# Scattering the expert rows into the result by an adding DMA, in place of a separate sum at the end of the program

## What is computed

```
logits = x_flat @ gate_w + gate_b;  gates = softmax(logits)
topk_gates, topk_idx = top_k(gates, 2);  topk_gates /= sum(topk_gates)
for e in range(8):
    h = gelu(x_flat @ w1[e] + b1[e]);  y = h @ w2[e] + b2[e]
    out = out + combine[:, e:e + 1] * y
t = t + out          # t: the tokens after the causal attention, "the residual"
```

## Time and profile before

| | us |
|---|---|
| median of three runs | 863.15 |
| lowest and highest of them | 858.99, 865.65 |
| time of the profiled execution | 858.26 |
| its span, first to last instruction | 856.4 |
| tile stage with TensorE full, about | 660 to 836 |
| behind the last scatter's issue | 836.1 to 856.4 |

### The profile page before, as it was taken

How to read it: one execution, slowest core, us unless ns; L and a number is a source line. 1 busy time by engine, 2 the same in 40 slices (tenths; PEclk the granted TensorE clock), 3 DMA queues, 4 the chain that set the end, 5 groups by cost and what they waited for, 6 DMA issues and landing times.

```text
span 856.4 us, 15650 instructions
## 1 busy us (share of the span) xinstructions
PE 737.3 (86%) x5694; PEld 647.3 (76%) x5694; DVE 448.4 (52%) x1073; ACT 333.1 (39%) x724; POOL 156.1 (18%) x306
## 2 busy tenths in 40 slices
PE   4688889989989988998998998878688999999990
PEld 3558778868868867886886887757577999999990
DVE  4355656857667683575767768353534222222213
ACT  6124354333433523344353452423273444444430
POOL 5010000121030220113103022012204121211210
PEclk9999999999999996899999998579798999999995
DMA  6702944931030212203012021955304111111117
GB/s 223 176 11 72 250 108 130 226 94 43 24 89 6 67 38 56 57 11 94 23 46 77 19 57 38 238 151 159 111 7 121 43 39 42 44 42 39 43 34 225
DMA packets 62049, 72.18 MB, mean 84 GB/s; under 512 B 6370, under 2 KB 52286, under 8 KB 61846
## 3 DMA queue, kind: packets, MB, share of 16 engines
q1 hardware_dynamic: 58566, 64.17, 27.7%
q0 software_dynamic: 3408, 7.02, 2.7%
HBM read 27.26 MB, written 23.17 MB: 59 GB/s over the span
## 4 chain that ended last, share of the span: by engine, by line
PE 73%; DVE 9%; DMA 6%; issue 5%; ACT 4%; SPq 1%; POOL 1%; another core or an unknown queue 1%; DVEq 0%; POOLq 0%; ACTq 0%
PE ps L2129 8%; PE ps L1819 7%; PE ps L2112 6%; PE ps L2113 6%; PE ps L1777 5%; PE ps L1778 5%; PE ps L1971 4%; PE ps L1944 4%; PE ps L1995 3%; PE ps L1896 3%; PE ps L1910 3%; DVE max_rows_a L1260 2%; PE ps L2034 2%; DMA q_rows_a<-max_at 2%; PE ps L1863 2%
## 5 line engine op out<-in xcount | busy, mean ns | idle before, releaser
L2112 PE MATMUL ps<-rows_t,w_tile 97*128 97x128 f32 x468 | 91.4, 276 | 3.3 <-DVE rows_t L1488 3.3
L2113 PE MATMUL ps<-rows_t,w_tile 96*128 96x128 f32 x468 | 90.5, 274 | 0.0
L2129 PE MATMUL ps<-w_exp,hid_t 128*128 x468 | 84.2, 331 | 2.3 <-DVE y_out L1496 1.4
L1479 DVE COPY w_tile<-w_exp 96x768 f32 x39 | 21.7, 556 | 120.3 <-PE ps L2113 102.1
L1328 DVE TENSOR_REDUCE max_b<-ps 128x3 f32<-128x384 f32 x96 | 48.6, 549 | 68.9 <-PE ps L2012 67.9
L1819 PE MATMUL ps<-s_q,rel_w 128*128 128x96 f32 x512 | 79.5, 314 | 3.0 <-DMA s_q<-staged_a 1.2
L2129 PEld LDWEIGHTS ps<-w_exp,hid_t 128*128 128x128 f32 x468 | 76.4, 193 | 3.5 <-issue 3.5
L1819 PEld LDWEIGHTS ps<-s_q,rel_w 128*128 128x128 f32 x512 | 74.3, 203 | 5.1 <-issue 2.7
L2112 PEld LDWEIGHTS ps<-rows_t,w_tile 97*128 97x128 f32 x468 | 72.4, 191 | 5.2 <-DVE rows_t L1488 5.1
L881 ACT ACTIVATE probs_a<-ps 98x392 f32<-98x392 f32 x96 | 47.9, 499 | 70.1 <-PE ps L1899 68.3
L2113 PEld LDWEIGHTS ps<-rows_t,w_tile 96*128 96x128 f32 x468 | 70.8, 191 | 0.0
(11 more groups left out here) (229 smaller groups left out, 1633.0 us busy)
## 6 DMA issues: line engine op xcount, KB each, us to landing
xs_dram<-blank SPq DMA_DIRECT2D x32, 388.0 KB, 8.6
w_exp<-in_e_w SPq DMA_DIRECT2D x16, 576.0 KB
ks_a<-staged_a SPq DMA_DIRECT2D x32, 192.0 KB
qs_b<-staged_b SPq DMA_DIRECT2D x32, 192.0 KB
ks_b<-staged_b SPq DMA_DIRECT2D x32, 192.0 KB
tile_x<-xs_dram SPq DMA_DIRECT2D x39, 97.0 KB
w_exp<-y_dram SPq DMA_DIRECT2D x8, 384.0 KB, 6.7
rel_w<-in_rel_tables SPq DMA_DIRECT2D x1, 1792.0 KB, 9.6
```

Of the source, the lines that this page charges most:

```text
L2112: pe.matmul(dst, w1_tile[t % 2][:, 0, cols], rows_t[t % 2][:, 0, :], start=True, stop=False)
L2113: ins = pe.matmul(dst, w1_tile[t % 2][0:DC, 1, cols], rows_t[t % 2][0:DC, 1, :], start=False, stop=True)
L2129: ins = pe.matmul(TILE_Y[:, 0:D], hid_t[t % 2][:, f, :], w_exp[:, bass.ds(e, 1), 2 * MLP + f * D:2 * MLP + (f + 1) * D].rearrange("p e d - ...
```

## The change

The scatter of each tile goes into `result` itself, with addition as the DMA's operation, and `result` has been filled with the residual by `store_t2`. Blank rows have a destination of 2048 or more and are left out by the DMA's bounds check. `t2_dram`, `y_dram`, `t2_all`, `tokens_in` and the whole end are gone. GpSimd's first scatter waits for the stores of the first seven images, and that of tile 21 for all eight. Since a tile must not be added twice, numbers beyond the end now lead to an extra blank tile of `xs_dram`, which takes a 33rd fill, and DVE's `table` does two more operations, for a second table `tile_row` that SyncE reads.

```
-                sp.dma_start(t2_dram[2 * i:2 * i + 2].rearrange("t p d -> p t d"), by_tile(x_4[:, :])).then_inc(t2_out, 16)
+                sp.dma_start(out[2 * i:2 * i + 2].rearrange("t p d -> p t d"), by_tile(x_4[:, :])).then_inc(t2_out, 16)
...
+                        sp.dma_start(xs_dram[NE * TOKENS:], blank[:, :]).then_inc(zero_out, 16)
...
-                at = sp.value_load(tile_at[0:1, t:t + 1], min_val=0, max_val=NE * REGION - 1)
+                at = sp.value_load(tile_row[0:1, t:t + 1], min_val=0, max_val=NE * REGION)
...
-            def tokens_in(t):
-                sp.wait_ge(t2_out, 16 * B)
-                sp.dma_start(t2_all[:, :, :], t2_dram.rearrange("t p d -> p t d")).then_inc(t2_in, 16)
...
-            for q in range(4):
-                for s in range(2):
-                    sp.dma_start(y_all[:, s, quarters[q], :], slots[s, :, quarters[q]]).then_inc(y_in[q], 16)
-            for q in range(4):
-                sp.wait_ge(mixed, q + 1)
-                sp.dma_start(out[quarters[q]].rearrange("t p d -> p t d"), t2_all[:, quarters[q], :]).then_inc(stored, 16)
-            sp.wait_ge(stored, 16 * 4)
+            sp.wait_ge(t2_out, 16 * B)
...
             def tile_out(t):
                 gp.wait_ge(y_sb, t + 1)
+                if t == 0:
+                    gp.wait_ge(t2_out, 16 * (B - 1))
+                if t == EARLY:
+                    gp.wait_ge(t2_out, 16 * B)
                 if t:
                     gp.wait_ge(y_sent[(t - 1) % 2], 16 * ((t - 1) // 2 + 1))
                 gp.indirect_dma_start(
-                    out=y_dram, out_offset=bass.IndirectOffsetOnAxis(
+                    out=out.rearrange("t p d -> (t p) d"), out_offset=bass.IndirectOffsetOnAxis(
                         ap=tile_x[t % RING][:, DEST:DEST + 1].bitcast(U32), axis=0),
-                    in_=y_out[t % 2][:, :], in_offset=None).then_inc(y_sent[t % 2], 16)
+                    in_=y_out[t % 2][:, :], in_offset=None, bounds_check=TOKENS - 1, oob_is_err=False,
+                    compute_op=ALU.add).then_inc(y_sent[t % 2], 16)
...
+                after(dv.tensor_scalar(tile_f[:, lo:hi], tile_f[:, lo:hi], float(NE * REGION), None, ALU.min))
+                dv.tensor_copy(tile_row[:, lo:hi], tile_f[:, lo:hi])
                 after(dv.tensor_scalar(tile_f[:, lo:hi], tile_f[:, lo:hi], float(NE * REGION - 1), None, ALU.min))
...
-            dv.wait_ge(t2_in, 16)
-            for q in range(4):
-                dv.wait_ge(y_in[q], 32)
-                now = slice(NT // 4 * q, NT // 4 * (q + 1))
-                after(dv.tensor_tensor(t2_all[:, now, :], t2_all[:, now, :], y_all[:, 0, now, :], ALU.add))
-                dv.tensor_tensor(t2_all[:, now, :], t2_all[:, now, :], y_all[:, 1, now, :], ALU.add).then_inc(mixed, 1)
```

More of the change, by code:

```diff
@@ L73, in build @@
     pad_scratch = nc.dram_tensor("pad_scratch", (2, DC, 2, WIN), F32, kind="Internal").ap()
-    t2_dram = nc.dram_tensor("t2_dram", (NT, P, D), F32, kind="Internal").ap()
-    xs_dram = nc.dram_tensor("xs_dram", (NE * TOKENS, ROW), F32, kind="Internal").ap()
-    y_dram = nc.dram_tensor("y_dram", (2 * TOKENS + P, D), F32, kind="Internal").ap()
+    xs_dram = nc.dram_tensor("xs_dram", (NE * TOKENS + P, ROW), F32, kind="Internal").ap()
     with ExitStack() as keep:
@@ L82, in sem, with layers @@
             return keep.enter_context(nc.semaphore(name))
-        layers(nc, a, pad_scratch, t2_dram, xs_dram, y_dram, ps, sem, out)
-def layers(nc, a, pad_scratch, t2_dram, xs_dram, y_dram, ps, sem, out):
+        layers(nc, a, pad_scratch, xs_dram, ps, sem, out)
+def layers(nc, a, pad_scratch, xs_dram, ps, sem, out):
     with ExitStack() as ctx:
@@ L157, in layers @@
         tile_at = sb("tile_at", [P, NTILE], I32)
+        tile_row = sb("tile_row", [P, NTILE], I32)
         NORMS = ("a", "m", "b", "g")
@@ L207, in layers @@
             y_out = two("y_out", [P, D])
-            t2_all = sb("t2_all", [P, NT, D])
             tile_x = [sb(f"tile_x{n}", [P, ROW]) for n in range(RING)]
-        y_all = w_exp[:, :, :].rearrange("p e n -> p (e n)")[:, 0:2 * NT * D].rearrange(
-            "p (s t d) -> p s t d", s=2, t=NT)
         slot_rows = probs_a[:, :, :, :].rearrange("p r e n -> p (r e n)")[:, 0:KEYS]
@@ L284, in layers @@
             "twinned", "scattered", "dve_step", "totalled", "tiles_known")
-        w_in, b2_in, t2_in, ones_row = sems("w_in", "b2_in", "t2_in", "ones_row")
+        w_in, b2_in, ones_row = sems("w_in", "b2_in", "ones_row")
         tile_in = [sem(f"tile_in{n}") for n in range(RING)]
@@ L289, in layers @@
             "rows_ps", "rows_sb", "w1_first", "w1_second", "h_ps", "h_sb", "y_ps", "b2_sb", "y_sb")
-        y_in, mixed, stored = [sem(f"y_in{n}") for n in range(4)], sem("mixed"), sem("stored")
         went_on = sem("went_on")
@@ L525, in last @@
                     store_t2(i)
-                tokens_in(0)
                 tile_rows(4)
@@ L567, in _ @@
                 sp.wait_ge(y_sent[u], 16 * ((NTILE + 1 - u) // 2))
-            slots = y_dram[0:2 * TOKENS].rearrange("(s t p) d -> s p t d", s=2, p=P)
-            quarters = [slice(NT // 4 * q, NT // 4 * (q + 1)) for q in range(4)]
-            for q in range(4):
-                for s in range(2):
-                    sp.dma_start(y_all[:, s, quarters[q], :], slots[s, :, quarters[q]]).then_inc(y_in[q], 16)
-            for q in range(4):
-                sp.wait_ge(mixed, q + 1)
-                sp.dma_start(out[quarters[q]].rearrange("t p d -> p t d"), t2_all[:, quarters[q], :]).then_inc(stored, 16)
-            sp.wait_ge(stored, 16 * 4)
+            sp.wait_ge(t2_out, 16 * B)
         @block.gpsimd
@@ L661, in go @@
                     if i == 0 and k == 0:
-                        gp.wait_ge(zero_out, 16 * FILLS)
+                        gp.wait_ge(zero_out, 16 * (FILLS + 1))
                     if k == 0:
@@ L1385, in route_constants @@
                     for slot in range(2):
-                        dv.tensor_scalar(by_slot[:, :, slot], steps[:, :], lane[:, :], float(slot * TOKENS), ALU.add, ALU.add)
-                    after(dv.tensor_scalar(dest_f[:, 4 * B:4 * B + 1], lane[:, :], float(2 * TOKENS), None, ALU.add))
+                        dv.tensor_scalar(by_slot[:, :, slot], steps[:, :], lane[:, :], 0.0, ALU.add, ALU.add)
+                    after(dv.tensor_scalar(dest_f[:, 4 * B:4 * B + 1], lane[:, :], float(TOKENS), None, ALU.add))
                     dv.tensor_copy(dest[:, :], dest_f[:, :]).then_inc(dest_set, 1)
```

## The result

The changed kernel takes **867.71 us** (median of 20 runs, 860.23 to 885.11) beside 859.14 us of the kernel before; the ratio of the two is **1.014, with a 95% interval of 1.011 to 1.018**. 846.7 us and "faster" had been forecast, with a range up to 864. The forecast was wrong in sign.

What follows compares the result with a forecast made beforehand. TensorE, busy 86% of 856.4 us, was taken as the bound. The sum -17.6 + 0.8 + 0.4 = -16.4, applied to the median of 863.15, gave 846.7 us; range 841 to 864.

Steps and rivals of the forecast that it cites:

- The end, -17.6: After the last scatter's landing: all loads, sums and stores go except 0.42 us of leaving the program, 17.6 us less.
- The landing, 3.1: Adding scatter, issue to landing (L): 2.3 us plain plus 0.8 for a reading phase; costs 0.8 once at the tail.
- The ring closes at L = 3.7: Tile stage, four buffers reused: TensorE waits for loaded tiles only once the scatter's landing time L reaches 3.7 us.
- two periods = 5.99 + L: Tile stage: transpose to scatter 3.17, landing L, 0.72 to the load's issue, 2.1 to its landing; against 9.7 us.
- the slack, 1.6 us: Tile stage, kernel before: tile 38's load lands about 1.6 us before TensorE starts its transpose, so the load waits for TensorE.
- rival 2: Tile stage: L between 3.7 and 5.0 gives part back, for instance 861 us at 4.4; chances 0.09 to 4.06, 0.13 beyond.
- Rival 1: Tile stage: slow adding scatter, GpSimd's strict order needing L + 0.3 per tile; worked case 916 us; chance 0.23 above L 5.0.
- The signs that I had named for a wrong L: Next profile: median landing above 3.7, scatter intervals grown by half the excess, TensorE's idle time ended by `tile_x`.
- The tightest place at the beginning: Tile 2's scatter behind image 7's: its buffer is full at 666.5, TensorE wants it at 667.69, 1.2 us of slack.
- The fill: SyncE's queue: one extra DMA of 97 KB in front of 32 larger ones, cost 0.
- the load of 1536 KB: In the middle, beside the routing of image 7: its removal was counted as no gain, 0.
- the 0.4 forecast: DVE's table: two more operations 0.21 us apart, +0.4 us, all on the path.

Runs made afterwards that it cites:

- no_end: Kernel before without its final loads, sums and stores, residual stored into the result, experts' rows missing: 847.9 us beside 861.67, ratio 0.990.
- plain_scatter: Changed kernel with the addition taken out of the scatter, bounds check kept: 855.13 us, kernel before beside it 861.67.
- ring8: Changed kernel with eight tile buffers instead of four: 852.69 us, kernel before beside it 861.67, ratio 0.9985.
- extra_fill: Kernel before with only the 33rd fill of xs_dram added: 859.49 us beside 859.97, ratio 0.9997.
- after_again: Changed kernel, unaltered, timed again in a later set: median 874.6 us of six runs, kernel before beside it 861.67.
- ring6: Changed kernel with six tile buffers instead of four: 846.05 us, kernel before beside it 859.97, ratio 0.985.

## Why the forecast was wrong, step by step

**The end, -17.6: the step "save the 0.42 of leaving the program" was wrong.** Behind the last scatter show only what ended last. GpSimd's drain of 7.07 us was in the trace, under the loads, and I hadn't looked for what the removed work covered. Measured: 20.3 - 7.6 = **12.7**, where the forecast had 16.8 with the 0.8 of the longer landing taken off. no_end shows it without the rest of the change.

**The landing, 3.1: near by luck, 0.4 too small.** Measured 3.5. Half of the added 1.2 us is the longer issue (1.55 for 0.96), which I had only named as a way to be wrong. The DMA slices of 0.2 us from 785 to 793 show the rest:

```profile
DMA  0000466000000968980000030000377200000000
GB/s 0 0 0 0 74 202 198 23 0 0 0 0 0 58 54 104 165 112 0 0 0 0 0 82 0 0 0 0 47 159 233 58 0 0 0 0 0 0 0 0
...
q0 software_dynamic: 144, 0.10, 12.2%
```

The scatter issued at 785.54 has its packets in slices 14 to 18, that is 1.0 us where the earlier trace rows had 0.6. So the packets take 0.4 us more, not the 0.8 of a whole load, and whether that is a phase of reading no trace shows. It makes 144 packets instead of 48, for the same 0.10 MB. The engines work 12.2% of 16 x 8 us = 15.6 us for this one, against 7.1%, or 9.1 us, for two before: 3.4 times as much for one scatter. The rule of the Trainium skill (Collectives: The Full Stack, in "The bandwidth ceiling"), which is stated there for a step of a collective, would have had twice as much. The trace disagrees on both sides: the stretch of packets grew 1.7 times, the engines' time 3.4 times.

**The ring closes at L = 3.7: the step that decided.** The measured L of 3.5 lay below that, where the prediction's own sum has -17.6 + 1.2 + 0.4 = -16.0 and no wait. Two terms were missing from "two periods = 5.99 + L". The first is 0.51 for the bounds check, an edit in the diff that I had given no price. It stands ahead of the issue, and so isn't part of L. The second is 0.75 for TensorE's register load. I measured the slack, 1.6 us, from the load's landing to the *transpose*, and took it for the slack of TensorE. But its sequencer has to be ahead of the matrix unit by the register load behind the transpose; once it is held at the transpose's wait, that load lies open. With both, two periods are 7.25 + L, and the ring closes at L = 9.70 - 7.25 = **2.45 us**, not 3.7. A plain scatter of 2.3 just passes (plain_scatter: 4.85); by this sum 0.15 us more is enough to close the ring. At 3.5 the sum gives 5.37, measured 5.34. Taking off 0.75, 0.5 and both gives 5.0, 5.12 and 4.85; measured were 5.04, 5.21 and 4.95.

**The mechanism of the loss is that of rival 2, the ring of buffers, at a threshold that lay elsewhere; more than the whole gain was given back.** Rival 1's order on GpSimd was put at L + 0.3; with the check's 0.5 it is the 4.3 us at which ring8 catches up, less than 4.85, so it is not the bound. The signs that I had named for a wrong L came in another form: intervals grew, but TensorE's idle time was not ended by `tile_x`.

**The smaller steps.** The tightest place at the beginning had been given 1.2 us of slack, enough for 0.8. There, at the transpose of tile 6, TensorE waited 1.30 us. Tile 2's scatter took 1.91 us to issue, and the load into its buffer was issued 4.54 us behind its start (682.66 to 687.20), not 3.04; and TensorE wanted the buffer sooner, 5.3 us behind that start (689.26 - 1.30 - 682.66) where the rows of before had 6.35. The fill was free (extra_fill), and no_end shows no gain from the load of 1536 KB. In the second table the row copy starts 0.60 us behind the first of the limiting operations (678.66 to 679.26), before 0.29: 0.3 of the 0.4 forecast.

**The new sum.** 181.70 - 165.20 = +16.5 in the 34 intervals, -12.7 at the end: +3.8 from tile 4 on (189.3 - 185.5; 3.3 in after_again). Ahead of it, from SyncE's load of the last row maxima into `qs_b` (620.23 and 641.47) to tile 4's scatter, it is 50.6 before and 52.3 after: +1.7. That makes +5.5, where -16.4 was forecast: 16.5 of the 21.9 us between them are the ring, 4.1 the end, and 1.3 lies ahead of tile 4, as much as TensorE's wait at tile 6. The medians say +8.6, the ratio +9 to +15, the means of all 20 runs +10.9 with 4.1 either way. **What is left, 3 to 10 us, by the means perhaps only 1, stays open.** In the profiled pair it lies in the image stages and goes with their granted clock (0.89 and 0.93). But kernels with the whole change had 0.93 too (ring6), and one without it had 0.90 (no_end), so I can't put it down to the change, nor to the missing idle time at the end. If the stretch from tile 4 on is taken off the mean time of each kernel (three runs above 900 us left out), what lies ahead of it is as long in no_end and in extra_fill as in the kernel before (-0.3 and +0.8), and between -0.9 and +9.2 us longer in the kernels that carry the change, with 4 to 8 either way. So neither the 33rd fill nor the residual's new place shows a cost, and the rest differs too much from kernel to kernel to be given a cause.

**The version that beats both.** The changed kernel with six or eight buffers: 0.985 (0.977 to 0.992) with six from four runs, 0.987 (0.982 to 0.991) and 0.9985 (0.994 to 1.003) with eight in two sets, of which the first gives GpSimd one wait more and the second shows no gain. From tile 4 on it is 14 us shorter than the kernel before, and 18 shorter than the changed one. The space is that of the `t2_all` that the change freed.

## What to carry to other kernels

Before you price a longer transfer, write down the whole loop from one reuse of its buffer to the next, with the waits as the *sequencers* meet them: slack up to the first matmul behind a wait is not slack if a register load stands behind it and has been running ahead. When work at the end of a program is removed, look in the trace for what ran beneath it, an engine's drain too; the end moves to the next cover, not to the last removed line. A ring that is less than a microsecond from closing (here 9.70 - 6.74 - 2.3 = 0.66, where the prediction had 1.4) turns a gain of 13 us into a loss. Two more buffers settle it, and one register load moved ahead of a wait takes 10 of the 16.5 us back.

## What the runs showed of the hardware that I had not expected

- An adding indirect scatter of 128 rows of 768 bytes occupies GpSimd for 1.55 us (plain: 0.96) and lands after 3.5 us (plain: 2.3), in 144 packets instead of 48.
- The bounds check adds 0.5 us between the releasing semaphore and the issue (0.78 to 0.80 against 0.27 to 0.28) and leaves the issue as it is (0.98 against 0.96).
- GpSimd's drain at the end of the program takes 7.1 us when it starts with a plain scatter, 7.65 with an adding one, and 5.9 when all has landed. In all eleven kernels without the old end, the span ends 0.2 to 0.3 us behind it.
- Adding scatters that wait for each other follow at 4.3 us (ring8). The last interval, behind a blank tile, is 3.6 there.
- The load of the expert number takes TensorE's sequencer 0.8 us, and 0.75 of it lies open once the sequencer is held by a wait.
